# A gated delta stage written out without a loop, and a routed stage's blanks and biases laid out anew

## The reference

```python
ys = _geglu(xf @ Ws1 + bs1) @ Ws2 + bs2                 # shared expert
logits = (xf @ Wr + br) / TAU
top_val, top_idx = jax.lax.top_k(logits, 2)             # 2 of E = 12 experts per token
w = one_hot(top_idx) weighted by softmax(top_val)
h = jnp.einsum('nd,edh->enh', xf, We1) + be1[:, None, :]
yE = jnp.einsum('enh,ehd->end', _geglu(h), We2) + be2[:, None, :]
return (ys + jnp.einsum('end,ne->nd', yE, w)).reshape(B, T, Dm)
```

## Time and profile before

| | |
|---|---|
| median of 3 runs (lowest, highest) | 3055.92 us (3052.26, 3056.61) |
| the profiled execution: time, span | 3057.68 us, 3055.9 us |
| mean granted TensorE clock | 0.857 |
| busy: TensorE, VectorE, ScalarE, GpSimd | 2376.6, 2214.9, 1278.8, 272.4 us |
| VectorE in tenths, 40 equal slices | 6999999999999999960034877777255657665465 |
| TensorE in tenths, same slices | 6677777777777777769947999999767766778677 |
| DMA engines in tenths, same slices | 4111101111111111011018999995000001110421 |
| delta stage | start to about 1361 us |
| routed stage | about 2858 us to the end |

### The profile page before, as it was taken

How to read it: one execution, slowest core, us unless ns; L and a number is a source line. 1 busy time by engine, 2 the same in 40 slices (tenths; PEclk the granted TensorE clock), 3 DMA queues, 4 the chain that set the end, 5 groups by cost and what they waited for, 6 DMA issues and landing times. The chain is left out here.

```text
span 3055.9 us, 65022 instructions
## 1 busy us (share of the span) xinstructions
PE 2376.6 (78%) x25365; PEld 1619.7 (53%) x25365; DVE 2214.9 (72%) x4056; ACT 1278.8 (42%) x2862; POOL 272.4 (9%) x280
## 2 busy tenths in 40 slices
PE   6677777777777777769947999999767766778677
PEld 5667666666666666643314666666322221222366
DVE  6999999999999999960034877777255657665465
ACT  3333333333333333332225777776411132556334
POOL 0000000000000000000031010100022311110242
PEclk9777787877777878789977999999978887999888
DMA  4111101111111111011018999995000001110421
GB/s 173 30 30 30 30 22 24 30 30 30 30 30 30 30 30 30 16 39 27 0 50 228 250 229 244 234 239 137 35 0 0 0 23 56 41 41 24 156 68 62
DMA packets 200028, 214.43 MB, mean 70 GB/s; under 512 B 32150, under 2 KB 185766, under 8 KB 194310
## 3 DMA queue, kind: packets, MB, share of 16 engines
q1 hardware_dynamic: 197353, 205.39, 25.7%
q0 software_dynamic: 2400, 4.95, 0.5%
HBM read 138.16 MB, written 74.74 MB: 70 GB/s over the span
## 5 line engine op out<-in xcount | busy, mean ns | idle before, releaser
L1274 DVE TENSOR_REDUCE ra_top<-ps 128x1 f32<-128x512 f32 x256 | 161.6, 684 | 96.0 <-PE ps L1078 95.7
L2557 DVE TENSOR_REDUCE dl_ZO<-dl_XP 128x64 f32<-128x128 f32 (+6 forms) x448 | 219.7, 490 | 15.4
L2553 DVE TENSOR_TENSOR dl_XP<-dl_ZO,dl_G 128x64 f32<-128x64 f32 (+6 forms) x448 | 194.6, 434 | 15.4
L1928 DVE TENSOR_TENSOR ps<-ps,da_window 128x192 f32<-128x192 f32 (+1 forms) x256 | 101.3, 396 | 122.3 <-PE ps L1657 117.9
L1772 ACT ACTIVATE da_AB<-ps 128x384 f32<-128x384 f32 x256 | 124.8, 492 | 146.9 <-PE ps L1634 143.2
L1195 ACT ACTIVATE ra_PT<-ps 128x512 f32<-128x512 f32 x256 | 137.0, 597 | 115.6 <-PE ps L1097 115.5
L1782 ACT ACTIVATE da_E<-ps,da_top 128x512 f32<-128x512 f32 x256 | 176.3, 688 | 17.3 <-DVE da_top L1931 16.9
L1931 DVE TENSOR_REDUCE da_top<-ps 128x1 f32<-128x512 f32 x256 | 177.0, 691 | 8.8
L1664 PE MATMUL ps<-ident,da_E 128*128 128x128 f32 x1024 | 169.0, 288 | 1.3 <-ACT da_E L1782 1.2
L1473 POOL MEMSET da_K<- 32x4096 f32 x2 | 7.1, 3574 | 1559.8 <-POOLq L82 1559.8
L2163 PE MATMUL ps<-X,dl_taps_q 128*128 (+1 forms) x1088 | 144.8, 299 | 0.0
(11 more groups left out here) (397 smaller groups left out, 5668.2 us busy)
## 6 DMA issues: line engine op xcount, KB each, us to landing
da_bands<-da_AB SPq DMA_DIRECT2D x128, 384.0 KB, 3.8
dl_Abc<-dl_ends SPq DMA_DIRECT2D x64, 512.0 KB, 6.2
da_window<-da_bands SPq DMA_DIRECT2D x128, 192.0 KB, 4.4
da_across<-da_bands SPq DMA_DIRECT2D x128, 192.0 KB, 4.5
da_parts<-da_split SPq DMA_DIRECT2D x64, 96.0 KB, 3.4
rf_We<-in_rf_We SPq DMA_DIRECT2D x1, 4608.0 KB, 23.2
da_K<-da_parts SPq DMA_DIRECT2D x16, 256.0 KB
da_Q<-da_parts SPq DMA_DIRECT2D x16, 256.0 KB
```

Source lines behind the costliest of these rows:

```text
L1274: eng.tensor_reduce(top[:, m % 2, u:u + 1], ps[:, score_bank(UNITS * m + u), :], AXX, ALU.max, negate=True).then_inc(s["maxima"], 1)
L2553: link(eng.tensor_tensor(XP[:, :, :, SB - t:], seen.unsqueeze(1).to_broadcast([P, 2, I, t + 1]), G[:, x:x + 2, keys][:, ::-1, :].unsqueeze ...
L2557: link(eng.tensor_reduce(ZO[:, to:to + 1 + (2 * I - 1) * CH:CH].rearrange("p (k i) -> p k i", k=2), XP[:, :, :, SB - 1 - t:], AXX, ALU.add))
```

## The change

In the delta stage the loop over passes 1 to 15 becomes a Python loop that writes the passes out, on SyncE, TensorE, ScalarE and VectorE: addresses and awaited values become constants, the jump back goes. In the routed stage the fill copies the same bytes by 128 pieces of 43 rows each (22360 bytes), where the access pattern so far named 5504 rows of 520 bytes. The biases `be1` are laid out by the host with the expert as the fastest index, so that L712 reads them in steps of one element and no longer of six.

```diff
-        yield [(s["loaded"], pairs), (s["filled"], [(slots, d["rf_blank"])]), (s["experts_loaded"], large)]
+        yield [(s["loaded"], pairs), (s["filled"], [(slots.rearrange("(p j) x -> p (j x)", p=P), d["rf_blank"].rearrange("(p j) x -> p (j x)", p=P))]), (s["experts_loaded"], large)]
...
-            own_bias = bias[:, 0:E * 2 * HR].rearrange("p (e m) -> p m e", e=E)
+            own_bias = bias[:, 0:E * 2 * HR].rearrange("p (m e) -> p m e", e=E)
...
             spread(0, 0)
             spread(0, 1)
-            with eng.Fori(1, NC) as n:
+            for n in range(1, NC):
                 spread(n, 0)
                 spread(n, 1)
...
             one_pass(0, True)
-            with eng.Fori(1, NC) as n:
+            for n in range(1, NC):
                 one_pass(n, False)
...
-        "rf_bias": columns(*(g[L3 + n] for n in ("be1", "bs1", "bs2"))),
+        "rf_bias": columns(g[L3 + "be1"].reshape(E, -1, P).transpose(1, 0, 2), g[L3 + "bs1"], g[L3 + "bs2"]),
```

More of the change, by code:

```diff
@@ L2707, in laid_out @@
         "rf_order": np.broadcast_to(100.0 - np.arange(E, dtype=np.float32), (P, E)),
-        "rf_be2": np.concatenate([g[L3 + "be2"], np.zeros((P - E, P), np.float32)]), "rf_bias": columns(*(g[L3 + n] for n in ("be1", "bs1", "bs2"))),
+        "rf_be2": np.concatenate([g[L3 + "be2"], np.zeros((P - E, P), np.float32)]), "rf_bias": columns(g[L3 + "be1"].reshape(E, -1, P).transpose(1, 0, 2), g[L3 + "bs1"], g[L3 + "bs2"]),
         "rf_Ws1": g[L3 + "Ws1"].reshape(P, -1, P), "rf_Ws2": rows_in(g[L3 + "Ws2"]),
```

## The result

The changed kernel took 3067.69 us (median of 6 runs, 3065.01 to 3070.41); the kernel before, beside it on the same chip, 3056.48 (3052.26 to 3058.88). The ratio is 1.0036, 95% interval 1.0023 to 1.0049: 11 us slower. The forecast was 3060.8 and its range ended at 3067.0.

The account below looks back on a forecast made before the run. VectorE's dependent chain, about 80.5 us a pass, was taken to bound the delta stage, GpSimd's scatters the routed stage's scatter. +5.1 + 2.1 - 2.3 = +4.9 us on 3055.9 gave 3060.8 us, range 3052.5 to 3067.

Parts of the forecast that it names:

- The clock of the first middles: Delta stage, L2195 before L2521: without jump stalls TensorE stands longer, its clock low in passes 2 to 15; +5.1 us.
- (a): Rival at L2195: the clock costs nothing, TensorE as often fast or slow as now; 3055.7 us, chance 0.18.
- (e): Rival at L2195: TensorE is fast everywhere, L2521's 8.4 us of waits go; 3047.3 us, chance 0.05.
- Waits against a constant: VectorE, L2497 to L2488: straight code takes 1.35 us instead of 1.28 at 30 places; +2.1 us.
- Program length: Delta stage: streaming the longer written-out programs costs nothing; taken 0, at most 13.5 us.
- rival (b): Delta stage: streaming stalls VectorE by 0.9 us in each pass; 3074.3 us, chance 0.10.
- The jumps: TensorE's 46.8 us of standing at fourteen loop jumps is off VectorE's chain, so removing it gains 0.
- rival (d): Delta stage: the loop jumps are on the path after all, saving 46.8 us; 3014.0 us, chance 0.03.
- The biases: Routed stage, L712: unit steps cut 5.71 to 3.38 us, releasing GpSimd's stretched scatter earlier; -2.3 us.
- Rival (c): Routed stage: the stretched scatter had another cause, or L712 keeps its rate; 3063.1 us, chance 0.08.
- The blanks: Routed stage's fill copy in long pieces: 16 us of cover before the scatters that wait for it; taken 0.

Follow-up runs that it names:

- pe_straight: Kernel before with only TensorE's delta loop written out; SyncE, ScalarE and VectorE keep theirs: 3081.80 us, ratio 1.0035.
- The fillers: Discarded TensorE identity products ahead of both middles' waits: in the changed kernel ratio 1.0027, in the looped kernel before with unit-step biases 1.0004.
- the moved products: Kernel before with L709, L712, L714 moved ahead of the routed stage's shared part: old bias order 3058.69 us, unit-step order 3055.17 us.
- both_steps: Kernel before with six discarded TensorE products ahead of each second middle, unit-step biases, and L709, L712, L714 moved ahead of the shared part: 3044.34 us, ratio 0.9966.
- offsets_first_new: Kernel before with unit-step biases and L709, L712, L714 moved ahead of the shared part, no discarded products: 3055.17 us, ratio 0.9997.
- fill_loop: Kernel before, loops kept, unit-step biases, 6 discarded TensorE products ahead of first middles and 8 ahead of second: 3073.44 us, ratio 1.0004.

## Why the prediction was wrong

*The clock of the first middles, +5.1: held.* The first middles grew by 4.2 us and L2521's waits to 13.7 us in 30 places (forecast: 12 in 32). With TensorE alone written out they grew by 3.8 (`pe_straight`); the rest is VectorE's own code, 2.74 us instead of 2.68 for a slow first middle. TensorE stands before W as foreseen, at the lower level; passes 4 and 2 of the changed kernel, and the stretch behind the first in the order of the earlier trace rows:

```profile
387.15 1.09 PE L2195 MATMUL ps<-ident,dl_W 128*128 128x128 f32 x4 [5.93 <-DVE dl_W L2547]
...
224.97 0.67 PE L2195 MATMUL ps<-ident,dl_W 128*128 128x128 f32 x4 [4.58 <-DVE dl_W L2547]
```

```profile
387.10:389.10 2.00, 1.11 (x6) 0.77 (x7) 1.93 (x5) 0.77 (x3) 0.00 (x0) 0.50 0.02 4
```

The rule "3.5 us of standing or more means 1.09 us" has exceptions: 4.58 us and yet 0.67 in pass 2, and the same in pass 6; on the other side 1.42 us of standing and yet 1.09, in the second middle of pass 12. How long TensorE stood does not settle it alone. The fillers confirm that the clock is what L2521 pays for, by taking it away. The rivals (a) and (e) fall.

*Waits against a constant, +2.1: held.* 28 places grew by 1.9 us, 1.28 to 1.35 each:

```profile
170.45 1.24 DVE L2497 STREAM_TRANSPOSE dl_Y<-ps 128x1024 f32<-128x1024 f32 x1
171.80 0.60 DVE L2488 TENSOR_TENSOR dl_XP<-dl_Y,dl_FB 128x256 f32<-128x256 f32 x1
```

*Program length, taken 0: this step failed.* It reasoned that "TensorE's code already streams" and that its stalls of 0.9 us in 4 places were known and harmless; the price of streaming was looked for on VectorE alone, which met none (rival (b) falls in the form it had). But where TensorE's stalls stand in a pass is a property of the loop: all passes share their code, so in the kernel before the four stalls came back at one product, and that product happened to be one with slack. Written out, a pass is 56 instructions more than a multiple of 256, and the places where stalls can stand walk through it. Two of them meet the last products of L2248, while VectorE stands waiting for these, and there they are 1.9 to 2.2 us long, not 0.9. These two passes give 4.5 of the 4.6 us of the second updates (2.5 to 5.0 in the four other kernels with the same TensorE program). 1.7 us more lie in the first updates and second middles, which differ by as much between executions, so how much of them the stalls make stays open.

The term should have been about 4.6 us and not 0. With it in the forecast's sum it is +9.5 us. The medians differ by 11.2 us and the two profiled executions by 7.8, so the rest is not accounted for to better than some 2 us.

The page "Runtime: NRT & Kernel Launch" of the Trainium skill, Instruction fetch mechanics, has the crossing from one block of code to the next mostly hidden and prefers full unrolling. No row here names the stalls' cause; that they are tied to the code's place and not to the chip agrees with fetching, and "mostly hidden" agrees with the many places that show no idle time. In time, though, unrolling TensorE's loop cost 10.7 us (`pe_straight`).

*The jumps, 0: held.* 46.8 us of standing went and nothing came back; rival (d) falls.

*The biases, -2.3: held.* L712 3.38 us as forecast, its scatter 3.10 (forecast: 3.1), L518 2.9 earlier after the first scatter. 2.35 us of these are this scatter. Another 0.43 are the scatter beside the mask, which took 1.39 us before and 0.96 now: it happened to start 0.11 us before the mask's end, too late to be held, which is luck and was not forecast. Rival (c) falls with the moved products.

*The blanks, 0: held as far as seen.* They landed 13.1 us after their issue at 2861.9, at 2875.0; the first scatter began at 2889.2. No kernel had this edit alone.

The sum of the profiled execution's own differences is +12.4 - 2.9 = 9.5; its span grew by 7.8. Stages that the change does not touch (the second to the seventh layer) move by up to 6 us either way between executions; here they take 2.8 us less together. Single terms below 2 us are therefore read from their places, not from the total.

## What to carry to other kernels

Before a loop is written out, list where each engine's "issue" stalls stand in the loop's body and what waits for the same engine elsewhere in the body: written out, they can come to stand before any of it. Count the instructions of a written-out body: here the remainder by 256 told by how much the stalls move from pass to pass. TensorE, where it runs dry just before it is needed, pays twice, once by the wait and once by its clock; six discarded products ahead of that one wait gave 10.8 us here (`both_steps` against `offsets_first_new`), while fillers ahead of both middles gave nothing (`fill_loop`). An instruction of VectorE with two inputs in SBUF should be timed by what GpSimd has to do beside it, not by VectorE's slack.

## What the runs showed of the hardware

- TensorE stood up to 2.5 us within a burst of 128 small products, ahead of the same product on four chips; 64 instructions more ahead of it moved the two stalls one pass earlier, 128 more left one above 1.5 us. All the places are a multiple of 256 instructions apart.
- TensorE starts an increment of a semaphore every 0.15 us: 128 of them from 7.2 to 26.6 us.
- A scatter of GpSimd that starts while VectorE multiplies two tensors in SBUF ends 0.82 to 0.84 us after the product (5.45 us beside 5.71, 3.10 beside 3.38); one already running kept its 0.96 us.
- The clock did not always fall while TensorE stood: after 4.58 and 4.59 us four transposes ran in 0.67 and 0.63 us in two places of the changed kernel; at the others with 3.5 us or more they took 1.08 to 1.09, and so they did once after 1.42.
- The kernel before takes 3055.4 to 3056.5 us on some chips and 3070.7 to 3072.4 on others; VectorE's long waits of 6.2, 7.7 and 9.0 us in the routed stage were seen only on the latter. The ratios of the changed kernel agree (1.0036, 1.0039).
